# Attention and feed-forward on one core: projections and transposed maxima in two passes of 64-row halves, with new orders on every engine

## The reference, cut to what matters

```python
x = L0_attn_x                                   # (16, 256, 256) f32
xn = layernorm(x)
qkv = xn @ w_qkv                                # 16 heads of 16
scores = einsum('bqhd,bkhd->bhqk', q / 4, k)    # causal, -1e10 above the diagonal
attn = softmax(scores)
out = einsum('bhqk,bkhd->bqhd', attn, v).reshape(b, s, 256)
ffn = qdot(gelu(qdot(xn, w_gating[0])) * qdot(xn, w_gating[1]), w_linear)   # fp8 operands
return x + out @ w_out + ffn
```

## Time and profile before

| what | value |
|---|---|
| median of 3 runs | 356.24 us |
| profiled execution, whole | 355.63 us |
| profiled execution, span of the profile | 353.9 us |
| attention stages s = 2 to 15, by the start of their first exponent scores | 136.0 to 336.1 us |
| what follows the last stage | 336.1 to 353.9 us |

### The profile page before, as it was taken

One profiled execution on the slowest core, in us unless ns is written; L12 is line 12 of the kernel. 1 busy time (PEld: TensorE's weight loads), 2 busy tenths in 40 slices (PEclk: granted clock), 3 DMA queues, 4 the chain that ended last, 5 costly groups with the idle time before them and its releaser, 6 DMA issues.

```text
span 353.9 us, 9788 instructions
## 1 busy us (share of the span) xinstructions
PE 335.8 (95%) x3514; PEld 256.5 (72%) x3514; DVE 298.9 (84%) x1359; ACT 227.3 (64%) x369; POOL 167.6 (47%) x203
## 2 busy tenths in 40 slices
PE   5998899999999989999999999999999999996996
PEld 5544455665676868788878888888888888884775
DVE  5888998998525778989989999899998999999765
ACT  1775677666655575776666766667667676775470
POOL 4104324132225264455565566654765557557461
PEclk9999999999999999999999999999999999999899
DMA  7969855773148342535528355284363652633011
GB/s 215 363 202 321 238 140 135 173 238 128 54 156 277 111 150 93 187 116 183 166 105 259 100 185 182 100 262 137 137 209 123 211 172 100 211 116 130 3 63 59
DMA packets 46569, 57.59 MB, mean 163 GB/s; under 512 B 2680, under 2 KB 39096, under 8 KB 46520
## 3 DMA queue, kind: packets, MB, share of 16 engines
q1 hardware_dynamic: 46520, 56.96, 50.2%
HBM read 16.78 MB, written 12.58 MB: 83 GB/s over the span
## 4 chain that ended last, share of the span: by engine, by line
PE 77%; DVE 12%; issue 3%; ACT 3%; DMA 2%; POOL 1%; SPq 1%; DVEq 0%; ACTq 0%; POOLq 0%
PE ps L841 12%; PE ps L950 12%; PE ps L928 10%; PE ps L901 8%; PE ps L848 7%; PE ps L828 6%; PE ps L805 6%; PE ps L971 5%; PE ps L811 5%; DVE masked L527 4%; PE ps L959 2%; DVE xn L429 2%; PE ps L788 2%; ACT gate L614 1%; DMA stack<-neg_max 1%
## 5 line engine op out<-in xcount | busy, mean ns | idle before, releaser
L527 DVE CUSTOM_DVE_ANT_0 masked<-ps,causal 128x256 bf16<-128x256 f32 (+1 forms) x512 | 148.3, 353 | 18.3 <-PE ps L901 18.2
L659 ACT ACTIVATE arena<-ps 128x1024 f32<-128x1024 f32 x96 | 98.2, 1027 | 54.6 <-PE ps L928 54.3
L363 POOL TENSOR_SCALAR_AFFINE_SELECT arena<-arena 128x512 f32<-128x512 f32 (+1 forms) x96 | 73.7, 788 | 33.9 <-ACT arena L659 33.7
L337 POOL TENSOR_TENSOR qk_part<-w_raw,qk_part 128x512 fp32r<-128x512 f32 x32 | 41.2, 1286 | 52.1 <-ACT qk_part L638 52.0
L614 ACT ACTIVATE gate<-ps 128x512 bf16<-128x512 f32 x64 | 38.5, 602 | 32.0 <-PE ps L805 31.4
L928 PE MATMUL ps<-stack 64*128 64x256 f32 (+1 forms) x512 | 51.6, 302 | 3.4 <-ACT arena L659 2.9
L841 PE MATMUL ps<-xs,wq_part 128*128 128x256 f32 x384 | 52.3, 285 | 0.4 <-ACT w_raw L632 0.3
L950 PE MATMUL ps<-arena,v_aug 128*32 128x256 f32 (+1 forms) x1024 | 49.5, 335 | 1.8 <-DVE o_norm L544 1.8
L901 PE MATMUL ps<-stack 63*128 63x256 f32 (+1 forms) x512 | 47.5, 284 | 1.8 <-DVE row_max L527 1.6
L841 PEld LDWEIGHTS ps<-xs,wq_part 128*128 128x128 f32 x384 | 47.5, 189 | 1.6 <-ACT w_raw L632 0.6
L928 PEld LDWEIGHTS ps<-stack 64*128 64x128 f32 x512 | 36.1, 187 | 16.3 <-issue 5.9
(11 more groups left out here) (64 smaller groups left out, 457.1 us busy)
## 6 DMA issues: line engine op xcount, KB each, us to landing
stack<-qk_part SPq DMA_DIRECT2D x96, 256.0 KB, 2.7
xs<-xt_store SPq DMA_DIRECT2D x16, 512.0 KB, 4.2
xt_store<-xt_part SPq DMA_DIRECT2D x14, 512.0 KB, 4.2
out_dram<-w_raw SPq DMA_DIRECT2D x15, 256.0 KB, 4.2
xres<-in_L_attn_x_dram SPq DMA_DIRECT2D x7, 512.0 KB, 6.7
arena<-in_L_ffn_w_gating_dram SPq DMA_DIRECT2D x2, 1024.0 KB, 8.9
stack<-zeros SPq DMA_DIRECT2D x4, 512.0 KB, 7.9
arena<-in_L_ffn_w_linear_dram SPq DMA_DIRECT2D x1, 1024.0 KB, 13.0
```

Of the source, the lines that this page charges most:

```text
L337: nc.gpsimd.tensor_tensor(qk_part[:, g, QLO:KLO + 1:3, :], qk_raw[:, g, :, :], qk_part[:, g, QHI:KLO, :].bitcast(F32), ALU.subtract).then_ ...
L363: nc.gpsimd.affine_select(diag, diag, pattern=[[0, 1024 // width], [1, P]], compare_op=ALU.is_ge, fill=0.0, base=0, channel_multiplier=-1) ...
L527: last = nc.vector.tensor_tensor_reduce(masked[:, place, i * width:(i + 1) * width], max_ps[:, place, i * width:(i + 1) * width], causal[: ...
L659: nc.scalar.activation(arena[:, n, :, :], exp_banks(b, n), ACT.Exp).then_inc(exp_done, 1)
```

## The change: what it does, and the diff

The projections of q, k, v (batches 3 to 15) and of the output (all but the last three batches), and most transposes of maxima, are done as two matmuls of 64 rows each in place of one of 128. The upper half of the rows writes one bank while the lower half writes the other (pass one); a second pass has the banks swapped, so that each output gets both halves added. Each second pass waits on a semaphore that the first pass raises; score units lie between. q/k, v and output projection now use both `misc` banks each, so they take turns in them. The transposed maxima move to the rotation of three banks, as one more place in it (`turns`); each place waits for the user three places earlier. The orders of all engines are rewritten, and `load_xs` on SyncE moves behind `place_max(s, 0)`.

```diff
+        def by_halves(b, c):
+            return b >= 2 and (b, c) != (B - 1, 1) or (b, c) == (1, 1)
+        turns = [("max", b, n, u) for b in range(2) for n in range(UNITS) for u in range(2)]
+        for b in range(2, B):
+            for n in range(UNITS):
+                turns += [("max", b, n, 0), ("max", b, n, 1)]
+                if n == 1:
+                    turns.append(("turned", b - 1, 1, 0))
+                if n == 3:
+                    turns.append(("turned", b, 0, 0))
+        turn = {k: i for i, k in enumerate(turns)}
+        def wait_for_turn(eng, key):
+            if turn[key] >= 3:
+                kind, b, n, u = turns[turn[key] - 3]
+                if kind == "max":
+                    eng.wait_ge(max_done, 2 * (UNITS * b + n) + u + 1)
+                else:
+                    eng.wait_ge(neg_done[n], b + 1)
+        def qk_bank(b, g):
+            return misc[:, :, 0:S] if b > 3 or (b, g) == (3, 1) else misc[:, 1, :].rearrange("p (a s) -> p a s", a=2)
...
 SyncE, stage s
-                if has(s + 3):
-                    load_xs(s + 3)
                 if has(s - 4):
                     store_y(s - 4)
                 if s >= 1 and has(s):
                     place_max(s, 0)
+                if has(s + 3):
+                    load_xs(s + 3)
...
 GpSimd, stage s (from 1)
+                if has(s + 1):
                     split_qk(s + 1, 0)
+                for n in range(5):
+                    mask(s - 1, n)
                 if has(s - 2):
                     split_ot(s - 2, 0)
+                mask(s - 1, 5)
+                if has(s + 1):
+                    split_qk(s + 1, 1)
+                if has(s - 2):
+                    split_ot(s - 2, 1)
...
 VectorE, stage s
+                if has(s - 2):
+                    o_to_rows(s - 2, 0)
                 if has(s - 1):
                     find_max(s - 1, 5)
-                if has(s - 2):
-                    o_to_rows(s - 2, 0)
-                    find_max(s, 0)
-                    find_max(s, 1)
+                find_max(s, 0)
                 if has(s - 2):
                     normalize_o(s - 2, 0)
-                    find_max(s, 2)
+                find_max(s, 1)
                 if has(s - 2):
                     o_to_rows(s - 2, 1)
-                    find_max(s, 3)
-                    find_max(s, 4)
+                find_max(s, 2)
+                find_max(s, 3)
                 if has(s - 2):
                     normalize_o(s - 2, 1)
                 if has(s - 3):
                     add_x(s - 3)
+                find_max(s, 4)
...
 ScalarE, stage s
+                if has(s + 1):
+                    copy_qk(s + 1, 1)
+                negate_max(s - 1, 1)
                 if has(s - 3):
                     round_ot(s - 3, 1)
+                exponent(s - 1, 1)
+                exponent(s - 1, 2)
                 if has(s + 1):
                     evacuate_v(s + 1)
                     round_qk(s + 1, 1)
+                exponent(s - 1, 3)
+                negate_max(s, 0)
+                round_ot(s - 2, 0)
+                exponent(s - 1, 4)
+                exponent(s - 1, 5)
                 if has(s + 2):
                     copy_qk(s + 2, 0)
...
 TensorE
+            def rows_of(r):
+                return slice(64 * r, 64 * r + 64)
+            def pass_qk(b, u, second):
+                if second:
+                    pe.wait_ge(qk_half[u], b - 3 + u)
+                elif u == 0:
+                    pe.wait_ge(xs_in[b % 2], 16 * (b // 2 + 1))
+                for i, (a, z, kt) in enumerate(TERMS):
+                    for r in range(2):
+                        s = 1 - r if second else r
+                        col = s * D + u * P
+                        last = nc.tensor.matmul(misc[:, s, 0:S], wq_part[rows_of(r), a, kt, col:col + P],
+                                                xs[b % 2][rows_of(r), z, kt, :], start=(i == 0 and not second),
+                                                stop=(i == len(TERMS) - 1 and second), skip_group_check=True)
+                last.then_inc(qk_ready[u] if second else qk_half[u], 1)
...
+            def pass_max(b, c, r):
+                if r == 0:
+                    pe.wait_ge(max_done, 2 * UNITS * b + UNITS * (c + 1))
+                    wait_for_turn(pe, ("turned", b, c, 0))
+                else:
+                    pe.wait_ge(maxt_half[c], b - 1 + c)
+                for t in range(QT):
+                    q = t * P + 64 * r
+                    last = nc.tensor.transpose(maxt_bank(b, c)[0:PAIRS, q:q + 64],
+                                               row_max[rows_of(r), b % 2, t, PAIRS * c:PAIRS * (c + 1)], ident[rows_of(r), rows_of(r)])
+                last.then_inc(maxt_ready[c] if r else maxt_half[c], 1)
...
             for s in range(2, B):
+                if s >= 3 and has(s + 1):
+                    pass_qk(s + 1, 0, True)
+                max_scores(s, 0)
+                exp_scores(s - 1, 0)
                 if has(s + 1):
                     pe.wait_ge(qk_copied[0], s + 2)
+                    pass_qk(s + 1, 1, False)
+                max_scores(s, 1)
                 if has(s + 1):
+                    pass_qk(s + 1, 1, True)
+                pass_max(s - 1, 1, 0)
+                exp_scores(s - 1, 1)
+                pass_max(s - 1, 1, 1)
+                times_v(s - 2, 1)
+                if has(s + 1):
+                    pe.wait_ge(qk_copied[1], s + 2)
+                    pass_v(s + 1, False)
+                max_scores(s, 2)
+                exp_scores(s - 1, 2)
+                if has(s + 1):
+                    pass_v(s + 1, True)
+                max_scores(s, 3)
+                pass_max(s, 0, 0)
                 if has(s - 3):
+                    pe.wait_ge(*((v_done, s + 2) if has(s + 1) else (y_done, s - 3)))
+                    pass_out(s - 3, 0, False)
+                exp_scores(s - 1, 3)
                 if has(s - 3):
+                    pass_out(s - 3, 0, True)
+                    pass_out(s - 3, 1, True)
+                pass_max(s, 0, 1)
+                max_scores(s, 4)
+                if has(s - 3):
+                    pass_out(s - 3, 1, False)
+                exp_scores(s - 1, 4)
+                times_v(s - 1, 0)
                 if has(s + 2):
+                    pe.wait_ge(*((y_done, s - 2) if has(s - 3) else (v_done, s + 2)))
+                    pass_qk(s + 2, 0, False)
+                max_scores(s, 5)
+                exp_scores(s - 1, 5)
```

More of the change, by code:

```diff
@@ L523, in find_max @@
                 for u in range(2):
[L524 removed]
+                    place = max_bank(b, n, u)
                     for i in range(heads):
@@ L888, in max_scores @@
             def max_scores(b, n):
-                unit = UNITS * b + n
                 st = stack[b % NB]
@@ L892, in max_scores @@
                     pe.wait_ge(stacked[n // 3], 48 * (b + 1))
-                if 2 * unit - 1 >= 1:
-                    pe.wait_ge(max_done, 2 * unit - 1)
+                for u in range(2):
+                    wait_for_turn(pe, ("max", b, n, u))
                 heads, qt = (4, 0) if n % 3 == 0 else (2, 1)
@@ new lines, in pass_v @@
+            def pass_v(b, second):
+                if second:
+                    pe.wait_ge(v_half, b - 2)
+                for i, (a, z, kt) in enumerate(TERMS):
+                    for r in range(2):
+                        t = 1 - r if second else r
+                        last = nc.tensor.matmul(misc[:, t, 0:D], xs[b % 2][rows_of(r), z, kt, t * P:(t + 1) * P],
+                                                wq_part[rows_of(r), a, kt, 2 * D:3 * D], start=(i == 0 and not second),
+                                                stop=(i == len(TERMS) - 1 and second), skip_group_check=True)
+                last.then_inc(v_ready if second else v_half, 1)
```

123 lines of the change are left out of this document (33 added, 90 removed).

## The result

The changed kernel is slower: 365.47 us (median of 4 runs, 362.02 to 368.08) against 355.78 for the kernel before on the same chips, a ratio of 1.025 [1.020, 1.030]. The prediction, 351.0 us with a range up to 356.5, was wrong in its sign. The profiled execution took 362.02 us, its span is 360.3, 6.4 us more than before. It was the fastest of the four, with TensorE's granted clock at 1.00; the other three had 0.972 to 0.989.

A forecast was written before the change was run, and what follows sets the result against it. TensorE paced the stages, with VectorE close behind and taking over after the change. Gains of 2.6 (eleven stages), 0.4 (late DMA), 0.3 (stage 2) and 1.2 (stages 14, 15) make 4.5 off 355.63: 351 us, range 344 to 356.5.

The forecast's parts named there:

- rival C: Second head half's stack lands too late for max 3: 0.3 to 0.5 us per stage, 355 to 356 us, chance 0.20.
- TensorE alone would need 12.9: TensorE's own time per stage: 14.31 less 1.5 for mode changes, plus 0.1 for short transposes, 12.9 us.
- The mode change: TensorE switching between 64 and 128 rows: 0.19 us each, eight fewer per stage, 1.5 us.
- a pass of six pairs: Twelve pass matmuls of 64 rows on TensorE: 0.70 us from start to start.
- The stage of 14.07: Hand schedule of one attention stage, VectorE idle 0.8 us and TensorE waiting 1.1: 14.07 us, 0.24 gained.
- Stage 2, "0.3": Stage 2, without output projection and held by VectorE: 0.3 us gained.
- Stages 14 and 15: Last two stages: 14 stays at 14.0, 15 runs at VectorE's 13.3 if the clock holds; 1.2 us gained.
- The tail: What follows stage 15 hangs on the last maxima and is unchanged.
- The late DMA in stage 4: The wait in stage 4 goes, as `load_xs` no longer stands before `place_max`: 0.4 us gained.
- Rival B: TensorE's pairs that add up cost more than score pairs, 0.14 us each: stage 14.8, 359 us, chance 0.10.
- Rival A: The stage's holes close: 13.25 at VectorE's floor, 342 us, or about 13.6, 346 us; chance 0.25.

The follow-up runs named there:

- e1: The changed kernel with GpSimd's subtraction for the second stack (`split_qk(s + 1, 1)`) behind mask 2 instead of mask 5: 359.41 us, ratio 1.012.
- j2: j1 with exp 3 ahead of the first output pass on TensorE: 348.96 us.
- j1: e5 with VectorE's search for the maxima reading only the first half of the columns: 350.25 us.
- e3: e1 with every pass of q, k, v and output as half as many matmuls of all 128 rows: 383.7 us.
- e2: e1 with VectorE's old order, max 5 ahead of the output's transpose, in stages 2 and 15 alone: 357.24 us, ratio 1.003.
- f1: The changed kernel with 34 no-ops added to TensorE's passes in each stage: 366.89 us.
- i1: e1 with SyncE's load of the next x back ahead of the store and the placing of the negated maxima: 357.46 us.
- f3: The changed kernel with 80 extra 8-column matmuls before the first real work, 288 records more: 396.41 us.
- f4: The changed kernel with 80 short transposes before the first real work, 16 warm-up ones less, 128 records more: 370.57 us.
- f2: The changed kernel with 144 short transposes before the first real work, 16 warm-up ones less, 256 records more: 379.52 us.
- e5: e2 with 28 throwaway transposes in TensorE's idle stretches of stages 2 and 15: 353.69 us, ratio 0.9965.

## Why the prediction was wrong, step by step

- **"Half a microsecond of air ... 0.3 to 0.5 per stage: 355 to 356 us" (rival C) is the step that failed, and with it the forecast's price of nothing for a late landing.** The mechanism was named, with its place and its air (measured 0.6: landing at 6.3, max 3 at 6.94; its own terms put the landing at 6.2, counted from the start of the third issue, and not at 6.5). The landing was taken from the page's median, 2.7. The trace of before holds landings of 4.4 to 4.6 for the same DMA, which cost nothing there, since they had several us of air; the price of a late one is 4.5 - 2.7 - 0.6 = 1.2 us, not 0.3 to 0.5. Against 14.22, five of the eleven stages are 0.8 to 1.4 too long and three more 0.1 to 0.4, 6.3 us in all; stage 14 lost another 0.7. e1 took both away. The forecast, which took no late landing, left it out, and the range's upper end was C's price with that size.
- **"TensorE alone would need 12.9".** With VectorE made lighter its chain takes 14.05 (j2) to 14.11 (j1), of which it is busy for 13.90 and 13.66. The mode change was counted at 0.19 and is worth 0.11 to 0.14 (e3); a pass of six pairs takes 0.71 in one place (258.09 to 258.80) and 0.81 in another (260.77 to 261.58); exp 1 with its four short transposes takes 0.53 where scores alone are 0.24. The new kernel's TensorE is 0.2 to 0.3 us a stage faster than the 14.31 before, not 1.4.
- **The stage of 14.07** measured 14.22 where nothing was late, every point within 0.22. The schedule was right, and half by luck: it took VectorE for the only bound, with TensorE 1.2 us behind, and the two are 0.1 apart. The gain per stage is 0.09 instead of 0.24, 1.0 us in eleven instead of 2.6.
- **Stage 2, "0.3".** It lost 1.0: VectorE's new order (the transpose of the output ahead of max 5) was not followed into stages 1 and 15, where the product with v comes late. e2: 1.7 and 0.5 us.
- **Stages 14 and 15, "1.2 ... if the clock holds".** The clock did hold in the kernel after (1.00 from 328.79 to 341.50), but the stretch gained only 0.5, as stage 14 lost 0.7 to the stack and 1.2 went at the start of stage 15, where max 0 waits for VectorE. The tail, called unchanged, lost 0.8; no run shows why. In f1, e1 and e2 the clock fell, in stage 2 as well, and took some 4 us of the profiled executions. No step had a price for the clock outside stage 15. The three other runs of the kernel after had a lower clock than the profiled one and took 2.2 to 6.1 us more; that they lost it in the same places is likely, but they left no trace.
- **The late DMA in stage 4, 0.4:** that wait is gone, and with it 0.5 us (14.84 before). But the move of `load_xs` was not the reason, or i1 would have it back.
- **Rival B** was rightly held small: six pairs in 0.71, 59 ns an instruction. **Rival A** rested on the 12.9: with TensorE at 14.05, no hole that closes brings a stage to 13.3 or 13.6.

With the measured sizes the sum of the profiled execution comes out: gained are 11 x 0.09 = 1.0 and stage 4's 0.5, lost 6.3 to the stack, 1.0 up to stage 2, 0.2 in stage 2 (13.87 for 13.67) and 0.3 behind stage 14's start (0.7 to the stack and 0.8 in the tail, less what was gained there): 353.9 - 1.5 + 7.8 = 360.2, the span within 0.1. The median, 365.47, has some 3 us more than this execution, the part that goes with the clock.

## What to carry to other kernels

Where a change takes the air from a DMA, count with the slowest landings in the trace, not the median: list them one by one, even those that nobody waited for. A saving on one engine is worth only the distance to the next chain, and a run in which the other engine is made lighter measures that distance better than any sum. Follow a new order into the first and the last rounds of the loop, and look there at the granted clock: here 28 throwaway transposes were worth 2.8 us, more than the 1.0 that the new order gained in eleven stages. And when one execution is profiled, see where it lies among the others: the fastest one hid what the clock cost here.

## What the runs showed that was not expected

- The instruction stream of TensorE is itself DMA traffic: one packet of 16 KB per about 256 records, and a data DMA that it meets lands in 4.0 to 4.8 us instead of 2.7. More, smaller instructions make such meetings more frequent (7.9 us instead of 9.8 apart).
- The same idle pieces don't always cost the clock: it fell in stage 2 of f1, f3 and f4, and not in the profiled execution of the kernel after, which has the same instructions there, nor in that of f2. It held in the last stage of the kernel after too, with TensorE idle for 2.4 of 12.7 us, and not in f1's. That idle pieces matter is shown by e5; what decides in a single execution is open.
- Scores with 128 columns take as long as those with 256: eight in 0.49 us (256.00 to 256.49), four in 0.24, so 60 ns an instruction of 64 rows in either case. The Trainium skill (TensorE: Matmul & The Clock Gate, in "Wait — 56ns, not 53.3ns?") gives 55.6 ns from start to start at 128 columns; by its formula, the columns at 2.4 GHz and some 2.5 ns more, an estimate for 256 is 109 ns. Here two halves run side by side: 60 ns an instruction agrees with that at 256 columns (half of 109 is 55), but not at 128, where half of 55.6 would be 28.
